# The last up unit of a routed block as three products of rounded high and low parts

## The chip, the cores and the metric

The kernel runs on one core of a Trainium2 chip. The metric is the device time of one execution, in microseconds; lower is better. A core has TensorE (matmuls; PE in the profile, with its weight loads as PEld), VectorE (DVE), ScalarE (ACT), GpSimd (POOL) and SyncE (SP), which here only issues DMAs. Each engine runs its own instructions in order and waits for others by semaphores.

## The reference, cut to what matters

A cross attention and a self attention come first, and then a feed-forward layer with experts on 512 tokens of width 512. Two shared experts see every token; of eight routed experts each token sees two.

```python
def _gelu(x):
    return jax.nn.gelu(x, approximate=False)
sh = _gelu(jnp.einsum('td,sdh->sth', xf, sW1) + sb1[:, None, :])
...
gates = xf @ rW + rb
topk_vals, topk_idx = jax.lax.top_k(gates, TOP_K)
...
h = _gelu(jnp.einsum('td,edh->eth', xf, W1) + b1[:, None, :])
y = jnp.einsum('eth,ehd->etd', h, W2) + b2[:, None, :]
moe = jnp.einsum('te,etd->td', w, y)
```

All of it is in float32. The kernel computes `h` and `y` only for the chosen pairs of token and expert, gathered into blocks of 128 rows of one expert each.

## The kernel before, in words

**Numbers.** TensorE takes float32 operands in two ways here. A plain float32 matmul is issued as two instructions, each with its own load of the stationary 128x128 tile. The other way uses the rounded type float32r (`F32R`), whose matmul is one instruction. To keep the precision, an operand is then split into a high part, the value cast to float32r, and a low part, the value less its high part, and a product is made of three terms: high by high, high by low, low by high. In the trace both kinds are printed as f32. Which is which is seen from the line and the tiles: `wsh`/`wsl`, `hh`/`hl`, `xAh`/`xAl`, `xBh`/`xBl`, `blk`, `wkh`/`wkl` and `wvh`/`wvl` are parts in float32r.

**Stages.** Attention fills the span up to about 770 us, then come the shared experts (lines 1146 and 1166, two passes over 256 tokens each), and from 971 us the routed blocks, one after the other, up to 1231 us. There can be up to `NBLK` = 15 blocks; `NE` = 8 are run always, the others behind a branch on the number of blocks, and this input runs 10.

**One routed block k.** Its 2 x 4 weight units of 1 MB each (128 partitions of 2048 floats) go through `ring`, eight buffers, of which unit n takes number n % 8. So up unit q of every block lies in buffer q, and down unit q in buffer 4 + q. SyncE loads them in the order up 0 to 3, down 0 to 3 (`load_block`, line 620), an up unit when PE has finished with that buffer's up unit of the block before (`ru_pe`), a down unit when DVE has split the one before (`wl_dve`).

- Up: for each unit q PE makes 4 output tiles of 4 matmuls (line 1285), stationary 128x128 pieces of the unit as they came in, moving the 128 gathered tokens `xg` (part of `xT`). ACT applies the GELU with the bias (line 1507), DVE splits the result into `hTh` and `hTl` (lines 2020, 2022). The up phase uses banks 0 and 1 in turn.
- Between: PE transposes the gathered rows of the next block (`turn_fetched`, line 1206), DVE copies them out of the bank into `xg` (`fetched`, line 1921).
- Down: for each unit q, 4 x 3 matmuls with 512 moving columns (line 1302), from `wsh`/`wsl`, the parts of the down unit: high by ACT (`weights_hi`, line 1378), low by DVE (`weights_split`, line 1721). ACT then scales the result (line 1518) into `yr`, or from block 7 on into `yh`.
- GpSimd only issues the indirect DMAs: it stores the rows of block k (`store`, line 843) and fetches the rows of block k + 3 (`fetch`, line 829). From block 8 on PE adds the block before into the result by a selection matmul (line 1263), behind up unit 0.

After block 6's rows are stored, SyncE reads all stored rows back, and only then loads the units of block 8.

Of the kernel before, what the change touches and what calls it, by code (L numbers as in the profile page):

```python
# [5 lines left out]
F32 = mybir.dt.float32  # L6
# [175 lines left out]
def build(nc, x, ctx, tails, wq, bq, wk, bk, wv, bv, wo, bo, ak, av, aq, ap_, abp, rw, rb,  # L182
          w1, b1, w2, b2, out):
    st = ExitStack()
    with st:
        def sb(name, shape, dt=F32):
            return st.enter_context(nc.sbuf_tensor(name, shape, dt))
# [111 lines left out]
        with ExitStack() as over:  # L299
# [28 lines left out]
        wsh2, wsl2 = sb("wsh2", [P, 2048], F32R), sb("wsl2", [P, 2048], F32R)  # L328
        ring1 = sb("ring1", [P, 2048])
        xBl = sb("xBl", [P, 4, 256], F32R)  # L330
        ring3 = sb("ring3", [P, 2048])
        xr = sb("xr", [P, 2, D])
        ring0, ring5 = sb("ring0", [P, 2048]), sb("ring5", [P, 2048])
# [10 lines left out]
        hTl = hl[:, :, :].rearrange("p a (b k) -> p (a b) k", b=4)  # L344
        yh = xAh[:, 0:2, :].rearrange("p b k -> p (b k)")
        yl = xAl[:, 0:2, :].rearrange("p b k -> p (b k)")

        xg = xT[:, 2:4, :].rearrange("p a (t k) -> p a t k", t=4)
        iotaw = xT[:, 0, :].bitcast(I32)
# [16 lines left out]
            "eps_dve iota_dve ones_dve cs_dve un_dve wkl_dve wvl_dve tl_dve kt_dve bias_dve xr_dve f_dve "  # L366
            "cr_dve bn_dve xn_dve xa_dve xt_dve sm_dve oh_dve nrm_dve xl_dve rt_dve hd_dve "
            "zero_dve wide_dve wl_dve xg_dve gt_dve rh_dve yl_dve add_dve last_dve sum_dve "
            "const_pool mask_pool iota_pool unit_pool cl_pool da_pool k2_pool bp_pool wide_pool xa_pool nm_pool wol_pool xl_pool wql_pool wsum_pool wsl_pool"
        ).split()  # L370
        s = {n: st.enter_context(nc.semaphore(n)) for n in names}
        bank_read = [st.enter_context(nc.semaphore(f"bank{i}_read")) for i in (0, 1, 7)]
# [3 lines left out]
        wq_in = [st.enter_context(nc.semaphore(f"wq{c}_in")) for c in range(2)]  # L376
        x_in = [st.enter_context(nc.semaphore(f"x{h}_in")) for h in range(2)]
        ring_in = [st.enter_context(nc.semaphore(f"ring{i}_in")) for i in range(NR)]
        b1_in = [st.enter_context(nc.semaphore(f"b1_{k}_in")) for k in range(NBLK)]

        pj = [bank[0], bank[1], bank[7]]
        uses = projections()
# [39 lines left out]
        def slot(n):  # L422
            return n % NR
# [61 lines left out]
        def sync(e):  # L485
# [133 lines left out]

            def load_block(k):  # L620
                ex = e.value_load(kint[0:1, k:k + 1], min_val=0, max_val=7)
                e.dma_start(b1r[:, k, :], b1[ex]).then_inc(b1_in[k], 16)
                for kind in (0, 1):
                    for q in range(4):
                        n = unit_routed(k, q, kind)
                        wait_slot(n)
                        e.dma_start(ring[slot(n)][:], (w1, w2)[kind][ex, q]).then_inc(ring_in[slot(n)], 16)
# [20 lines left out]
        def pool(e):  # L648
# [172 lines left out]
            def fetch(k):  # L821

                if k == 0:
                    e.wait_ge(s["rt_dve"], RT_TAB)
                    e.wait_ge(s["rows_in"], 64)
                    e.wait_ge(s["pr_pe"], 4)
                elif k >= 2:
                    e.wait_ge(s["tg_pe"], k - 1)
                e.indirect_dma_start(xr[:, k % 2, :], None, xrows,
                                     bass.IndirectOffsetOnAxis(ap=tabi[:, 0, k:k + 1], axis=0)).then_inc(s[("even_in", "odd_in")[k % 2]], 16)  # L830

            def fetch_rest(k):
                if k < NBLK:
                    with e.If(blocks > k - 1):
                        fetch(k)
                        fetch_rest(k + 1)

            def store(k):

                e.wait_ge(s["yh_act"], k + 1)  # L840
                if k == 0:
                    e.wait_ge(s["yz_in"], 16)
                e.indirect_dma_start(yrows, bass.IndirectOffsetOnAxis(ap=tabi[:, 1, k:k + 1], axis=0), yr[:, k % 2, :],  # L843
                                     None).then_inc(s[("even_out", "odd_out")[k % 2]], 16)

            for k in range(3):
                fetch(k)
            for k in range(NDIR):
                store(k)
                if k + 3 <= NE:  # L850
                    fetch(k + 3)
            fetch_rest(NE + 1)

        def pe(e):
            def warm(n, dst):
# [341 lines left out]
            def turn_fetched(k):  # L1197
                e.wait_ge(s[("even_in", "odd_in")[k % 2]], 16 * (k // 2) + 16)
                if k == 0:
                    e.wait_ge(s["wT_act"], 1)  # L1200
                elif k == 1:
                    e.wait_ge(s["ge_act"], 2 * NSH)
                else:
                    e.wait_ge(s["xg_dve"], k)
                for c in range(4):
                    m = e.transpose(bank[3 if k else 1][:, P * c:P * c + P], xr[:, k % 2, P * c:P * c + P], ident[:])
                m.then_inc(s["tg_pe"], 1)
# [60 lines left out]
            def routed(k):  # L1268
                y = k % 2
                for q in range(4):  # L1270
                    un = unit_routed(k, q, 0)
                    if q == 1 and k > NDIR:
                        e.wait_ge(s["yl_dve"], k - NDIR)
                        e.wait_ge(s["gt_dve"], k - NDIR)
                        scattered("sc_pe")
                    if 4 * k + q >= 2:
                        e.wait_ge(s["rg_act"], 4 * k + q - 1)
                    else:
                        e.wait_ge(s["rt_dve"], RT_POS)
                    e.wait_ge(ring_in[slot(un)], ring_value(un))  # L1280
                    if q == 0:
                        e.wait_ge(s["xg_dve"], k + 1)
                    for jj in range(4):
                        for c in range(4):
                            m = e.matmul(bank[q % 2][:, P * jj:P * jj + P],  # L1285
                                         ring[slot(un)][:, 512 * c + P * jj:512 * c + P * jj + P], xg[:, y, c, :],
                                         start=(c == 0), stop=(c == 3))
                    m.then_inc(s["ru_pe"], 1)
                if k + 1 < NBLK:
                    turn_fetched(k + 1)  # L1290
                if k == 0:
                    e.wait_ge(s["ge_act"], 2 * NSH)
                elif k <= NDIR:
                    e.wait_ge(s["yh_act"], k)
                for q in range(4):
                    r_ = 32 + 4 * k + q
                    e.wait_ge(s["rh_dve"], 2 * (4 * k + q) + 2)
                    e.wait_ge(s["wl_dve"], r_ + 1)
                    for jj in range(4):
                        j = 4 * q + jj  # L1300
                        for x_, (h_, w_) in enumerate(((hTh, wsh), (hTh, wsl), (hTl, wsh))):
                            m = e.matmul(bank[2][:], h_[:, j, :], w_[r_ % 3][:, 512 * jj:512 * jj + 512],  # L1302
                                         start=(j == 0 and x_ == 0), stop=(j == 15 and x_ == 2))
                    m.then_inc(s["rd_pe"], 1)
# [13 lines left out]
        def act(e):  # L1318
# [172 lines left out]
            e.wait_ge(s["rt_dve"], RT_INT)  # L1491
            blocks = e.value_load(kint[0:1, 15:16], min_val=0, max_val=NBLK)

            def routed(k):
                y = k % 2
                for q in range(4):
                    if q < 3:
                        weights_hi(32 + 4 * k + q)
                    n = 4 * k + q
                    e.wait_ge(s["ru_pe"], n + 1)  # L1500
                    if n >= 2:
                        e.wait_ge(s["rh_dve"], 2 * (n - 2) + 2)
                    if q == 0:
                        e.wait_ge(b1_in[k], 16)
                    for jj in range(4):
                        j = 4 * q + jj
                        m = e.activation(hg[:, q % 2, P * jj:P * jj + P], bank[q % 2][:, P * jj:P * jj + P], ACT.Gelu,
                                         bias=b1r[:, k, j:j + 1])
                    m.then_inc(s["rg_act"], 1)
                weights_hi(32 + 4 * k + 3)  # L1510
                e.wait_ge(s["rd_pe"], 4 * k + 4)
                if k == 0:
                    e.wait_ge(s["tab_in"], 16)
                elif 2 <= k <= NDIR + 1:
                    e.wait_ge(s[("even_out", "odd_out")[k % 2]], 16 * (k // 2))
                if k > NDIR:
                    e.wait_ge(s["sc_pe"], k - NDIR)
                e.activation(yr[:, y, :] if k < NDIR else yh, bank[2][:], ACT.Identity, scale=tab[:, k, 1:2]).then_inc(s["yh_act"], 1)  # L1518

            def rest(k):  # L1520
                if k < NBLK:
                    with e.If(blocks > k):
                        routed(k)
                        rest(k + 1)

            for k in range(NE):
                routed(k)
            rest(NE)
# [11 lines left out]
        def vector(e):  # L1540
# [375 lines left out]
            def fetched(k):  # L1916
                y = k % 2
                e.wait_ge(s["tg_pe"], k + 1)
                if k >= 2:
                    e.wait_ge(s["ru_pe"], 4 * (k - 2) + 4)  # L1920
                e.tensor_copy(xg[:, y, :, :],
                              bank[3 if k else 1][:].rearrange("p (c k) -> p c k", c=4)).then_inc(s["xg_dve"], 1)

            for n in range(NSLOT):
                i, d = part_of(n) if n < NCH else (NPART, 0)
# [115 lines left out]
            def rest(k):  # L2041
                if k < NBLK:
                    with e.If(blocks > k):
                        routed(k)
                        rest(k + 1)
# [70 lines left out]
```

## Time and profile before

| | |
|---|---|
| time, median of 3 runs | 1240.17 us (1238.33 to 1241.58) |
| the profiled execution's own time | 1241.11 us |
| its span, first to last instruction | 1239.4 us |
| mean granted TensorE clock | 0.991 |
| PE busy | 1210.2 us, 98% of the span |
| DVE, ACT, POOL busy | 68%, 55%, 46% |
| DMA queues of weights and data | 172.42 MB, 38.0% of 16 engines over the span |

The shares are means over stages with different limits; POOL, for instance, is busy in the attention and nearly idle in the last quarter. The difference of 1.7 us between time and span lies outside the profiled instructions.

### The profile page before, as it was taken

The page shows a single profiled execution, that of the slowest core. Times are in us where ns is not written, and L with a number is a line of the kernel's source. Part 1 is how long each engine was busy: PE and PEld are TensorE (multiplying, and loading weights), DVE is VectorE, ACT ScalarE, POOL GpSimd, SP SyncE. Part 2 cuts the span into 40 slices and gives each one's busy share as a digit, 9 for nine tenths or more (in the row PEclk, how much of TensorE's full clock was granted, in tenths as well). Part 3 has the DMA queues.
Part 4 walks back from the last instruction along what each step waited for, and adds up shares of the span by engine and source line. Part 5 has one row for each costly group of instructions (what it writes and reads, how often), then busy time and mean ns, then how long its engine had stood idle before and what let it go on. Part 6 is the DMA issues. An engine that isn't in the chain of part 4 may idle for free.

```text
span 1239.4 us, 33792 instructions
## 1 busy us (share of the span) xinstructions
PE 1210.2 (98%) x14478; PEld 1133.6 (91%) x14478; DVE 839.8 (68%) x1265; ACT 687.0 (55%) x1236; POOL 571.7 (46%) x357
## 2 busy tenths in 40 slices
PE   8999999999999999999999998999999999999998
PEld 7899999989999989999989997898889999999997
DVE  7666786776777686786785875766676455555655
ACT  4366656745755655756656557555644445544443
POOL 5656767776758776867766764000041001000000
PEclk9999999999999999999999998899999999999999
DMA  7331111121121212012112123745455599999991
GB/s 268 121 105 40 41 40 37 44 73 67 41 82 39 76 70 70 23 67 74 41 70 74 36 107 146 306 172 179 170 191 208 192 362 345 346 338 354 355 384 36
DMA packets 34794, 179.40 MB, mean 145 GB/s; under 512 B 6264, under 2 KB 9496, under 8 KB 15568
## 3 DMA queue, kind: packets, MB, share of 16 engines
q1 hardware_dynamic: 32896, 172.42, 38.0%
q0 software_dynamic: 1744, 4.76, 1.2%
q8 instruction: 117, 1.92, 0.6%
q14 instruction: 37, 0.30, 0.1%
HBM read 168.97 MB, written 8.19 MB: 143 GB/s over the span
## 4 chain that ended last, share of the span: by engine, by line
PE 91%; DVE 4%; issue 2%; POOL 1%; ACT 1%; DMA 0%; DVEq 0%; SPq 0%; POOLq 0%
PE bank L928 18%; PE bank L931 18%; PE bank L1285 12%; PE sc L1302 9%; PE sc L951 7%; PE sc L1146 7%; PE bank L970 4%; PE sc L1166 4%; PE bank L1166 4%; PE bank L909 1%; PE bank L1037 1%; DVE tt L1623 1%; POOL xn L731 1%; PE bank L1091 1%; PE bank L996 1%
## 5 line engine op out<-in xcount | busy, mean ns | idle before, releaser
L731 POOL TENSOR_TENSOR xn<-xn,tt 128x1024 f32<-128x1024 f32 x96 | 231.9, 2416 | 165.1 <-DVE tt L1623 163.3
L931 PE MATMUL bank<-wvh,blk 128*128 128x256 f32 x1344 | 248.8, 287 | 5.3 <-DVE va L1594 5.3
L928 PE MATMUL bank<-blk,wkh 128*128 128x256 f32 x1344 | 246.0, 285 | 0.0
L1721 DVE TENSOR_TENSOR wsl<-ring,wsh 128x2048 fp32r<-128x2048 f32 x72 | 165.2, 2294 | 112.6 <-ACT wsh L1378 109.8
L1442 ACT ACTIVATE tt<-sc 128x512 f32<-128x512 f32 (+1 forms) x208 | 107.8, 603 | 217.1 <-PE sc L951 209.3
L931 PEld LDWEIGHTS bank<-wvh,blk 128*128 128x128 f32 x1344 | 209.9, 192 | 8.8 <-DVE va L1594 6.1
L928 PEld LDWEIGHTS bank<-blk,wkh 128*128 128x128 f32 x1344 | 209.2, 192 | 4.2 <-issue 1.6
L931 PE MATMUL bank<-wvl,blk 128*128 128x256 f32 x672 | 190.6, 284 | 0.0
L928 PE MATMUL bank<-blk,wkl 128*128 128x256 f32 x672 | 190.0, 283 | 0.0
L1378 ACT CAST wsh<-ring 128x2048 fp32r<-128x2048 f32 x72 | 137.4, 1909 | 45.8 <-PE sc L1302 21.2
L1285 PEld LDWEIGHTS bank<-xT,ring 128*128 128x128 f32 x1280 | 144.8, 192 | 1.0
L1285 PE MATMUL bank<-xT,ring 128*128 128x128 f32 x1280 | 144.8, 275 | 0.0
L1623 DVE SCALAR_TENSOR_TENSOR tt<-sc,tt 128x512 f32<-128x512 f32 (+1 forms) x208 | 132.9, 680 | 0.8 <-ACT tt L1455 0.8
L931 PEld LDWEIGHTS bank<-wvl,blk 128*128 128x128 f32 x672 | 129.4, 193 | 0.0
L928 PEld LDWEIGHTS bank<-blk,wkl 128*128 128x128 f32 x672 | 128.8, 192 | 0.0
L685 POOL TENSOR_TENSOR blk<-bsum,blk 128x512 fp32r<-128x512 f32 x96 | 124.1, 1321 | 6.1 <-DVE bsum L1572 4.8
L1451 ACT ACTIVATE tt<-tt 128x512 f32<-128x512 f32 (+1 forms) x208 | 121.2, 644 | 0.0
L1455 ACT ACTIVATE tt<-tt 128x512 f32<-128x512 f32 (+1 forms) x208 | 120.9, 643 | 0.0
L951 PEld LDWEIGHTS sc<-qc,kk 32*128 32x128 f32 x3072 | 91.7, 189 | 11.9 <-DVE tt L1623 4.3
L951 PE MATMUL sc<-qc,kk 32*128 32x64 f32 x3072 | 98.3, 276 | 4.1 <-DVE tt L1623 4.1
L685 POOL TENSOR_TENSOR blk<-stg,blk 128x512 fp32r<-128x512 f32 x72 | 97.1, 1362 | 1.8 <-ACT blk L1330 1.8
L843 POOL DMA_INDIRECT yrows<-xT,tabi x7 | 6.9, 988 | 193.2 <-ACT xT L1518 193.2
(327 smaller groups left out, 2204.9 us busy)
## 6 DMA issues: line engine op xcount, KB each, us to landing
ring<-in_w SPq DMA_DIRECT2D x112, 1024.0 KB, 6.1
stg<-in_ctx SPq DMA_DIRECT2D x24, 1024.0 KB, 5.0
wqt<-in_wo SPq DMA_DIRECT2D x4, 1024.0 KB, 5.0
wqt<-in_aq SPq DMA_DIRECT2D x4, 1024.0 KB, 5.0
wqt<-in_ap_ SPq DMA_DIRECT2D x4, 1024.0 KB, 4.9
yrows<-K SPq DMA_DIRECT2D x1, 2048.0 KB, 12.4
bsum<-in_tails SPq DMA_DIRECT2D x2, 520.0 KB, 6.6
ktail<-bsum SPq DMA_DIRECT2D x1, 1040.0 KB, 4.1
```

The source lines that it names most:

```text
L685: e.tensor_tensor(block_lo(i, j), block_raw(i, j), block_hi(i, j).bitcast(F32), ALU.subtract).then_inc(s["cl_pool"], 1)
L731: e.tensor_tensor(dacc[0:kn, y, :], dacc[0:kn, y, :], tt[0:kn, w, :], ALU.add).then_inc(s["da_pool"], 1)
L928: m = e.matmul(dst[:, 256 * a:256 * a + 256], w[:, WPOS[j], c, r], x[:, c, :], start=(k_ == 0), stop=(k_ == 5))
L931: m = e.matmul(dst[:, 256 * a:256 * a + 256], x[:, c, r], w[:, WPOS[j], c, :], start=(k_ == 0), stop=(k_ == 5))
L951: m = e.matmul(sc[0:kn, h, c0 + 64 * g:c0 + 64 * g + 64], key, qc[r, g, 64 * b:64 * b + 64], start=True, stop=True)
L1285: m = e.matmul(bank[q % 2][:, P * jj:P * jj + P], ring[slot(un)][:, 512 * c + P * jj:512 * c + P * jj + P], xg[:, y, c, :], start=(c == 0) ...
L1302: m = e.matmul(bank[2][:], h_[:, j, :], w_[r_ % 3][:, 512 * jj:512 * jj + 512], start=(j == 0 and x_ == 0), stop=(j == 15 and x_ == 2))
L1378: e.copy(wsh[m % 3][:], ring[slot(un)][:]).then_inc(s["wh_act"], 1)
L1451: e.activation(tt[0:kn, w, r], tt[0:kn, w, r], ACT.Ln, bias=1.0).then_inc(s["ln_act"], 1)
L1455: e.activation(tt[0:kn, w, r], tt[0:kn, w, r], ACT.Exp, scale=-1.0).then_inc(s["ex_act"], 1)
L1623: e.scalar_tensor_tensor(t_, score_read(n, kn, hb), 0.0, t_, ALU.max, ALU.add).then_inc(s["f_dve"], 1)
L1721: e.tensor_tensor(wsl[m % 3][:], ring[slot(unit_split(m))][:], wsh[m % 3][:].bitcast(F32), ALU.subtract).then_inc(s["wl_dve"], 1)
```

## The change

In every routed block the last up unit (q = 3) is multiplied in three terms of float32r parts, where it was one plain float32 product. Three things are made for that.

- The high part of the unit, `uph`, by ACT: two casts of 128x1024 into `xBh` and `xBl`, the buffers of the shared experts' second pass (`up_hi`). For blocks below 8 it is made one block ahead, behind the cast of down unit 3; for block 0 at the start of the stage; for blocks 8 and later at the start of the block itself.
- The low part, `upl`, by GpSimd: two subtractions of 128x1024, written over ring buffer 3 itself, in which the raw unit lies (`up_lo`). GpSimd does it for block k + 1 ahead of the store of block k.
- The parts of the 128 gathered tokens, `xgh` and `xgl`, by DVE from the bank, behind the copy into `xg`, which the units 0 to 2 still use.

The bias loads of the blocks take two semaphores, by the block's parity, in place of fifteen.

```diff
+            upl = over.enter_context(nc.sbuf_tensor("upl", [P, 2048], F32R))
         ring3 = sb("ring3", [P, 2048])
...
+        xgh, xgl = (w[:, 2:4, :].rearrange("p a (t k) -> p (a t) k", t=2) for w in (xAh, xAl))
+        uph = [w[:, :, :].rearrange("p c k -> p (c k)") for w in (xBh, xBl)]
...
-                e.dma_start(b1r[:, k, :], b1[ex]).then_inc(b1_in[k], 16)
+                e.dma_start(b1r[:, k, :], b1[ex]).then_inc(b1_in[k % 2], 16)
...
+            def up_lo(k):
+
+                e.wait_ge(s["uph_act"], k + 1)
+                for h in range(2):
+                    c = slice(1024 * h, 1024 * h + 1024)
+                    m = e.tensor_tensor(upl[:, c], ring[slot(unit_routed(k, 3, 0))][:, c], uph[h].bitcast(F32), ALU.subtract)
+                m.then_inc(s["upl_pool"], 1)
...
+            up_lo(0)
+            for k in range(NE):
+                if k + 1 < NE:
+                    up_lo(k + 1)
+                if k < NDIR:
+                    store(k)
                 if k + 3 <= NE:
                     fetch(k + 3)
...
                     if q == 0:
-                        e.wait_ge(s["xg_dve"], k + 1)
+                        e.wait_ge(s["xg_dve"], 3 * k + 1)
+                    elif q == 3:
+                        e.wait_ge(s["xg_dve"], 3 * k + 3)
+                        e.wait_ge(s["upl_pool"], k + 1)
                     for jj in range(4):
+                        dst = bank[q % 2][:, P * jj:P * jj + P]
                         for c in range(4):
...
+                            if q < 3:
+                                m = e.matmul(dst, ring[slot(un)][:, col], xg[:, y, c, :], start=(c == 0), stop=(c == 3))
+                                continue
+                            hi = uph[c // 2][:, 512 * (c % 2) + P * jj:512 * (c % 2) + P * jj + P]
+                            for x_, (w_, x__) in enumerate(((hi, xgh), (hi, xgl), (upl[:, col], xgh))):
+                                m = e.matmul(dst, w_, x__[:, c, :], start=(c == 0 and x_ == 0), stop=(c == 3 and x_ == 2))
...
+            def up_hi(k):
+
+                un = unit_routed(k, 3, 0)
+                e.wait_ge(ring_in[slot(un)], ring_value(un))
+                for h in range(2):
+                    m = e.copy(uph[h], ring[slot(un)][:, 1024 * h:1024 * h + 1024])
+                m.then_inc(s["uph_act"], 1)
...
                 weights_hi(32 + 4 * k + 3)
+                if k + 1 < NE:
+                    up_hi(k + 1)
                 e.wait_ge(s["rd_pe"], 4 * k + 4)
...
+                e.tensor_copy(xg[:, y, :, :], src).then_inc(s["xg_dve"], 1)
+                e.tensor_copy(xgh, src).then_inc(s["xg_dve"], 1)
+                e.wait_ge(s["xg_dve"], 3 * k + 2)
+                e.tensor_tensor(xgl, src, xgh.bitcast(F32), ALU.subtract).then_inc(s["xg_dve"], 1)
```

On TensorE, at the up phase of block 1, the order before is (each row is a line, an operation, the tile written and the tiles read, the moving shape and a count):

```order
L1302 MATMUL sc<-wsh,hl 128x512
L1285 MATMUL bank<-xT,ring 128x128 x64
L1206 MATMUL sc<-ident,xr 128x128 x4
L1302 MATMUL sc<-wsh,hh 128x512
L1302 MATMUL sc<-wsl,hh 128x512
```

And of the change, at the same place (its lines 1309, 1313, 1224 and 1328 are the plain up matmuls, the new ones, the transposes and the down matmuls):

```order
L1328 MATMUL sc<-wsh,hl 128x512
L1309 MATMUL bank<-xT,ring 128x128 x48
L1313 MATMUL bank<-xAh,xBh 128x128
L1313 MATMUL bank<-xAl,xBh 128x128
L1313 MATMUL bank<-xAh,upl 128x128
...
L1224 MATMUL sc<-ident,xr 128x128 x4
L1328 MATMUL sc<-wsh,hh 128x512
```

The three new rows stand 16 times in all (with `xBl` in the place of `xBh` for half of them): the last 16 of the 64 plain matmuls are gone, and 48 of float32r stand in their place, still 128 moving columns wide.

On ScalarE, in block 0, from the cast of down unit 3 into block 1, before:

```order
L1507 ACTIVATE hr<-bank,K 128x128 x8
L1378 CAST wsh<-ring 128x2048
L1518 ACTIVATE xT<-sc,tab 128x512
L1378 CAST wsh<-ring 128x2048
L1507 ACTIVATE hr<-bank,K 128x128 x4
```

And of the change:

```order
L1543 ACTIVATE hr<-bank,K 128x128 x8
L1404 CAST wsh<-ring 128x2048
L1525 CAST xBh<-ring 128x1024
L1525 CAST xBl<-ring 128x1024
L1556 ACTIVATE xT<-sc,tab 128x512
L1404 CAST wsh<-ring 128x2048
```

The two casts of `up_hi` for block 1 have come in ahead of the scaling of block 0's result.

On GpSimd, behind the three fetches that open the stage, before:

```order
L829 DMA xr<-xrows,tabi 128x512 x3
L843 DMA yrows<-xT,tabi 2944x512
L829 DMA xr<-xrows,tabi 128x512
L843 DMA yrows<-xT,tabi 2944x512
L829 DMA xr<-xrows,tabi 128x512
```

And of the change:

```order
L833 DMA xr<-xrows,tabi 128x512 x3
L857 TENSOR_TENSOR upl<-ring,xBh 128x1024
L857 TENSOR_TENSOR upl<-ring,xBl 128x1024
L857 TENSOR_TENSOR upl<-ring,xBh 128x1024
L857 TENSOR_TENSOR upl<-ring,xBl 128x1024
L849 DMA yrows<-xT,tabi 2944x512
L833 DMA xr<-xrows,tabi 128x512
```

The subtractions for blocks 0 and 1 now stand ahead of the store of block 0, and so on by one pair for each block.

## Rows read from the trace of the kernel before

**Rows 1.** The page: busy us of each engine, and the chain that ended last by line.
```profile
PE 1210.2 (98%) x14478; PEld 1133.6 (91%) x14478; DVE 839.8 (68%) x1265; ACT 687.0 (55%) x1236; POOL 571.7 (46%) x357
PE bank L928 18%; PE bank L931 18%; PE bank L1285 12%; PE sc L1302 9%; PE sc L951 7%; PE sc L1146 7%; PE bank L970 4%; PE sc L1166 4%; PE bank L1166 4%; PE bank L909 1%; PE bank L1037 1%; DVE tt L1623 1%; POOL xn L731 1%; PE bank L1091 1%; PE bank L996 1%
```

**Rows 2.** The chain in order of time, blocks 1 and 8: start us, length us, count.
```profile
996.87 14.29 PE bank L1285 x128
1011.16 0.44 PE sc L1206 x4
1011.60 10.93 PE sc L1302 x48
...
1176.49 3.57 PE bank L1285 x32
1181.93 10.72 PE bank L1285 x96
```

**Rows 3.** Busy time in block 1: length, engines, granted clock, DMA share.
```profile
core 0: us, PE busy (x) PEld busy (x) DVE busy (x) ACT busy (x) POOL busy (x), PEclk, DMA share, GB/s
996.87:1022.53 25.66, 25.66 (x183) 23.74 (x182) 14.01 (x13) 12.52 (x21) 1.96 (x2) 1.00 0.92 349
```

**Rows 4.** Groups by line and shape, the up matmuls: busy us, mean ns.
```profile
L1285 PE MATMUL bank<-xT,ring 128*128 128x128 f32 x1280 | 144.8, 275 | 0.0
```

**Rows 5.** Chain: float32r matmuls 256 columns wide in the shared experts.
```profile
925.96 2.75 PE bank L1166 x12
928.71 2.87 PE sc L1146 x24
```

**Rows 6.** Timeline of weight loads: start, us, out<-in, stationary shape, count.
```profile
374.11 0.98 PEld L1014 LDWEIGHTS bank<-rwt,xaT 128*128 128x128 f32 x8
375.01 0.30 PEld L928 LDWEIGHTS bank<-blk,wkh 128*128 128x128 f32 x2
...
884.42 0.17 PEld L1181 LDWEIGHTS bank<-sel,ones 128*128 128x128 bf16 x4
...
6.93 0.66 PEld L857 LDWEIGHTS bank<-ones 128*128 128x128 bf16 x11
...
1011.33 0.19 PEld L1302 LDWEIGHTS sc<-wsh,hh 128*128 128x128 f32 x1
1011.44 0.19 PEld L1302 LDWEIGHTS sc<-wsl,hh 128*128 128x128 f32 x1
```

**Rows 7.** The weight loads of line 1181: ns min/median/max.
```profile
L1181 PEld LDWEIGHTS bank<-sel,ones x4: 95/96/96, 884.4 to 884.5; 128*128 128x128 bf16 x4
```

**Rows 8.** Timeline of ACT and DVE, block 1, between up and down.
```profile
1013.45 0.68 DVE L1921 COPY xT<-sc 128x512 f32<-128x512 f32 x1
1014.46 1.91 ACT L1378 CAST wsh<-ring 128x2048 fp32r<-128x2048 f32 x1 [2.12 <-PE sc L1302]
1016.40 2.29 DVE L1721 TENSOR_TENSOR wsl<-ring,wsh 128x2048 fp32r<-128x2048 f32 x1 [2.28 <-ACT wsh L1378]
1022.57 0.69 ACT L1518 ACTIVATE xT<-sc,tab 128x512 f32<-128x512 f32 x1 [6.20 <-PE sc L1302]
```

**Rows 9.** Prices from other stages: an ACT cast, DVE and POOL operations.
```profile
L1413 ACT CAST woh<-wqt 128x1024 fp32r<-128x1024 f32 x2 | 2.0, 1038 | 0.0
L1639 DVE TENSOR_TENSOR xTl<-sc,xTh 128x512 fp32r<-128x512 f32 x4 | 2.6, 681 | 0.2 <-ACT xTh L1346 0.2
L731 POOL TENSOR_TENSOR xn<-xn,tt x96: 2347/2405/4258, 78.2 to 771.9; 128x1024 f32<-128x1024 f32 x88, 65x1024 f32<-65x1024 f32 x8
```

**Rows 10.** Ring loads, issue to landing: 990 to 1050, then 1150 to 1185 us.
```profile
DMA to landing us min/median/max: 4.8/6.4/8.1
...
DMA to landing us min/median/max: 6.6/11.0/14.1
```

**Rows 11.** Timeline of POOL in block 2, and of ACT in block 8.
```profile
1023.53 0.99 POOL L843 DMA_INDIRECT yrows<-xT,tabi  x1 [23.40 <-ACT xT L1518]
...
1179.81 1.91 ACT L1378 CAST wsh<-ring 128x2048 fp32r<-128x2048 f32 x1 [2.60 <-DMA ring<-in_w]
```

More of the change, by code:

```diff
@@ L330, in build @@
         xBl = sb("xBl", [P, 4, 256], F32R)
+        with ExitStack() as over:
+            upl = over.enter_context(nc.sbuf_tensor("upl", [P, 2048], F32R))
         ring3 = sb("ring3", [P, 2048])
@@ L368, in build @@
             "zero_dve wide_dve wl_dve xg_dve gt_dve rh_dve yl_dve add_dve last_dve sum_dve "
-            "const_pool mask_pool iota_pool unit_pool cl_pool da_pool k2_pool bp_pool wide_pool xa_pool nm_pool wol_pool xl_pool wql_pool wsum_pool wsl_pool"
+            "const_pool mask_pool iota_pool unit_pool cl_pool da_pool k2_pool bp_pool wide_pool xa_pool nm_pool wol_pool xl_pool wql_pool uph_act upl_pool wsum_pool wsl_pool"
         ).split()
@@ L378, in build @@
         ring_in = [st.enter_context(nc.semaphore(f"ring{i}_in")) for i in range(NR)]
-        b1_in = [st.enter_context(nc.semaphore(f"b1_{k}_in")) for k in range(NBLK)]
+        b1_in = [st.enter_context(nc.semaphore(f"b1_{k}_in")) for k in range(2)]
         pj = [bank[0], bank[1], bank[7]]
@@ L830, in fetch, with rest @@
                                      bass.IndirectOffsetOnAxis(ap=tabi[:, 0, k:k + 1], axis=0)).then_inc(s[("even_in", "odd_in")[k % 2]], 16)
-            def fetch_rest(k):
+            def rest(k):
                 if k < NBLK:
-                    with e.If(blocks > k - 1):
-                        fetch(k)
-                        fetch_rest(k + 1)
+                    with e.If(blocks > k):
+                        if k + 1 < NBLK:
+                            fetch(k + 1)
+                        up_lo(k)
+                        rest(k + 1)
             def store(k):
@@ L844, in store @@
                                      None).then_inc(s[("even_out", "odd_out")[k % 2]], 16)
+            def up_lo(k):
[4 more added lines that the diff above has]
+                m.then_inc(s["upl_pool"], 1)
             for k in range(3):
                 fetch(k)
-            for k in range(NDIR):
-                store(k)
+            up_lo(0)
[4 more added lines that the diff above has]
+                    store(k)
                 if k + 3 <= NE:
                     fetch(k + 3)
-            fetch_rest(NE + 1)
+            rest(NE)
         def pe(e):
@@ L1203, in turn_fetched @@
                 else:
-                    e.wait_ge(s["xg_dve"], k)
+                    e.wait_ge(s["xg_dve"], 3 * k)
                 for c in range(4):
@@ L1281, in routed @@
                     if q == 0:
-                        e.wait_ge(s["xg_dve"], k + 1)
+                        e.wait_ge(s["xg_dve"], 3 * k + 1)
+                    elif q == 3:
+                        e.wait_ge(s["xg_dve"], 3 * k + 3)
+                        e.wait_ge(s["upl_pool"], k + 1)
                     for jj in range(4):
+                        dst = bank[q % 2][:, P * jj:P * jj + P]
                         for c in range(4):
-                            m = e.matmul(bank[q % 2][:, P * jj:P * jj + P],
-                                         ring[slot(un)][:, 512 * c + P * jj:512 * c + P * jj + P], xg[:, y, c, :],
-                                         start=(c == 0), stop=(c == 3))
+                            col = slice(512 * c + P * jj, 512 * c + P * jj + P)
+                            if q < 3:
[4 more added lines that the diff above has]
+                                m = e.matmul(dst, w_, x__[:, c, :], start=(c == 0 and x_ == 0), stop=(c == 3 and x_ == 2))
                     m.then_inc(s["ru_pe"], 1)
@@ L1492, in act @@
             blocks = e.value_load(kint[0:1, 15:16], min_val=0, max_val=NBLK)
+            def up_hi(k):
[4 more added lines that the diff above has]
+                m.then_inc(s["uph_act"], 1)
             def routed(k):
                 y = k % 2
+                if k >= NE:
+                    up_hi(k)
                 for q in range(4):
@@ L1503, in routed @@
                     if q == 0:
-                        e.wait_ge(b1_in[k], 16)
+                        e.wait_ge(b1_in[k % 2], 16 * (k // 2 + 1))
                     for jj in range(4):
@@ L1524, in rest @@
                         rest(k + 1)
+            up_hi(0)
             for k in range(NE):
@@ L1920, in fetched @@
                     e.wait_ge(s["ru_pe"], 4 * (k - 2) + 4)
-                e.tensor_copy(xg[:, y, :, :],
-                              bank[3 if k else 1][:].rearrange("p (c k) -> p c k", c=4)).then_inc(s["xg_dve"], 1)
+                src = bank[3 if k else 1][:].rearrange("p (c k) -> p c k", c=4)
+                e.tensor_copy(xg[:, y, :, :], src).then_inc(s["xg_dve"], 1)
+                e.tensor_copy(xgh, src).then_inc(s["xg_dve"], 1)
+                e.wait_ge(s["xg_dve"], 3 * k + 2)
+                e.tensor_tensor(xgl, src, xgh.bitcast(F32), ALU.subtract).then_inc(s["xg_dve"], 1)
             for n in range(NSLOT):
```

## The prediction

> **What bounds the kernel now.** I read the page first. TensorE is busy 98% of the span, and the chain that ended last lies on it almost throughout; lines 1285 and 1302, the up and down matmuls of the routed blocks, hold 12% and 9% [rows 1]. The chain in order of time then shows how a block is made up: 14.29 us of up matmuls, 0.44 us of transposes, 10.93 us of down matmuls, one behind the other without a gap, 25.66 us in all [rows 2]. The busy times of block 1 say the same from the other side: PE 25.66 of 25.66 us at a granted clock of 1.00, which is 2.4 GHz, while DVE works 14.01, ACT 12.52 and POOL 1.96 us [rows 3]. So a microsecond more or less on TensorE counts once for every block, and work on the other engines counts only if it makes TensorE wait. 1280 up instructions [rows 4] at 128 to a block [rows 2] are 10 blocks. One thing stands near: the DMA engines are busy 0.92 of a block, moving 349 GB/s [rows 3]. A much shorter block would meet that; a longer one loosens it.
>
> **What TensorE loses and gains.** An up phase has 128 instructions in 14.29 us, 111.6 ns each, so unit 3, a quarter of them (16 matmuls of two instructions), takes 3.57 us. In its place come 48 float32r matmuls, 128 columns wide, each with its own load of a 128x128 stationary tile. No such matmul is in the trace: its float32r matmuls are 256 wide or wider. Their rates are the nearest rows. 24 matmuls 256 wide take 2.87 us, 119.6 ns each; 12 that are 512 wide take 2.75 us, 229 ns each [rows 5]; 48 in a down phase take 10.93 us, 228 ns [rows 2]. The step from 256 to 512 columns costs 108 ns, that is 2.4 columns a ns, and about 12 ns are left over for each matmul. By that line alone 128 columns would take 53 + 12 = 65 ns. The 48 would take 3.1 us, and a block would win 0.45 us.
>
> [...] The gate's matmuls on line 1014 have only 8 moving columns, next to nothing to stream. Still their eight loads go from 374.11 to the next line's start at 375.01, 0.90 us, or 112 ns for each [rows 6]. So for a plain float32 tile the load is the bound, at 112 ns, which is also the 111.6 ns of the up phase. Is it the same for float32r? The first two loads of a down phase, float32r tiles with nothing in front of them, start 110 ns apart, at 1011.33 and 1011.44, while the later ones follow the matmuls' 228 ns [rows 6]. So a float32r tile, four bytes an element too, loads at 110 ns, and the loads, not the 53 ns of streaming, should set the pace of the new unit. bf16 tiles show how else it could be: four loads of a 128x128 bf16 tile end 0.17 us after the first began [rows 6] and last 0.095 us each [rows 7], so they start 25 ns apart; the eleven of line 857, for matmuls 128 wide, take 0.66 us, (0.66 - 0.10) / 10 = 56 ns apart [rows 6].
>
> Bounds for one new matmul with a load as the bound: 110 ns from the two loads, below; 119.6 ns above, the 256-wide float32r rate, since half the columns can't take longer. I take 112 ns, the pace of a chain that is seen to be bound by loads. It is nearest in what sets it; the 119.6 ns contain 107 ns of streaming, which the new unit has not. Then the unit takes 48 x 0.112 = 5.38 us, 1.80 us more than 3.57, and 10 blocks take **18.0 us** more. With 110 ns it is 48 x 0.110 - 3.57 = 1.71, 17.1 us; with 119.6 ns 5.74 - 3.57 = 2.17, 21.7 us.
>
> The Trainium skill, in TensorE: Matmul & The Clock Gate, section Back-to-back issue gap, states about 81 ns for each pair of a load and a matmul with 128 columns in a stream. By it the unit would take 3.89 us and the change cost 3.2 us. The trace has 112 ns where a four-byte tile is loaded, and I go by that.
>
> **ACT.** A cast of 128x1024 takes 1.04 us [rows 9], so `up_hi` adds 2.1 us to 12.52 of a block. In block 1 the cast of down unit 3 ends at 1016.37, and ACT idles 6.20 us before it scales the result at 1022.57 [rows 8]. There it waits for the next block's unit 3. SyncE can issue that load when the up phase ends, at 1011.16, and loads land 4.8 to 8.1 us after issue [rows 10]: at 1019.3 at the latest. The two casts end by 1021.4, before 1022.57. Cost nothing. If the load came more than 1.2 us later than that, the scaling, the next block's first cast and its first GELU would slip; but that GELU is needed only when the third up unit wants its bank, 7.1 us into the block.
>
> **GpSimd.** A subtraction of 128x1024 takes 2.4 us [rows 9], two 4.8. From 1021.4 they end by 1026.2; unit 3 of the next block is due at 1022.53 + 10.7 = 1033.2 by the old times. 7 us of cover. Behind them on GpSimd stand the store of the block's rows, issued at 1023.53 now [rows 11], up to 2.7 us later then, and the fetch for two blocks on. The store's reader is the reuse of `yr` two blocks later. The last one matters more: SyncE reads all rows back after store 6 and has the loads of block 8 behind that. There ACT waits 2.60 us for the ring, and casts the first down unit only at 1179.81 [rows 11], 3.3 us into block 8; the landings take up to 14.1 us [rows 10]. In blocks 8 and 9 `up_hi` comes ahead of that cast. If its unit landed only with the down unit, ACT would be done with it at 1181.9 and GpSimd at 1186.7; unit 3 is due at 1181.93 + 7.15 = 1189.1. The down unit's cast would end at 1183.8, and the first GELU, 1.14 us, at 1184.9, where the third up unit needs its bank at 1181.93 + 3.57 = 1185.5. It just fits, and each earlier block being longer gives loads more time. I put 0 here, with 1 us at most.
>
> **DVE.** Two operations follow the copy at 1013.45, a cast and a subtraction from a bank of 0.68 us each [rows 8, 9]. They end near 1015.5; the split of down unit 3 starts at 1016.40, held by ACT's cast [rows 8]. Nothing, with 0.9 us of cover; beyond it down unit 3, which comes at 1011.60 + 8.2 = 1019.8, has 1.1 us more behind the split's end at 1018.7. Block 0's operations fall in the shared experts, where TensorE is the bound too.
>
> **Semaphores and SyncE.** SyncE's order of loads is the same, and the parity wait asks for a load that was issued a block earlier. Nothing.
>
> Sum: 1241.11 + 18.0 = 1259.1 us against the profiled execution; that lies 0.9 above the median of the runs, so the median becomes **1258 us**.
>
> **Rivals.**
>
> *The load is hidden, and the change is faster.* If float32r tiles load faster in a row than the one pair shows, the unit goes by its streaming: 65 ns by the line above, 0.45 us won a block, 1235.7 us; with the 56 ns of the bf16 chain 2.69 us, 0.88 won, 1231.4 us. It decides below 74 ns a matmul, where 48 equal 3.57 us. For it: 12 + 53 fits every wider matmul. Against: the 110 ns pair, the 112 ns of line 1014. Chance 0.07. With the page's 81 ns it would be 1243.4 us, inside what a measurement can tell from no change; 0.03.
>
> *A narrow float32r matmul has a price that the wide ones don't show.* If it took as long as the two instructions of a plain float32 product, 223 ns, the unit would take 10.7 us, 7.1 more a block, 1312 us. Nothing in the trace speaks for it, and nothing is narrow enough to exclude it. 0.05.
>
> *The parts come late.* TensorE at its first new matmul waits for GpSimd. It costs what the chain ring, ACT, GpSimd exceeds 7 us of cover by, or 2.4 us in block 8. If GpSimd were three times as slow beside DVE (a single 4.26 us in [rows 9] is the slowest of 96), 2 x 7.2 = 14.4 us are 2.6 us over, 10 blocks 26 us, 1284 us. 0.03.
>
> **How the numbers follow.** The load-bound case has 0.82 and its own range from 1257 (110 ns) to 1263 us (119.6 ns, with the 1 us of block 8). About 0.3%, 3.7 us, is what a measurement tells from no change. Faster is the hidden load, 0.06 of its 0.07, since at 65 ns the gain is near that bound; the same 0.04; slower 0.90. The range: 1253 to 1266 us, which takes the load-bound case with 3 us to spare on either side for unpriced seams, and leaves out the others, 0.18.
>
> **What would show each step.** The new matmuls' group: 48 in 5.4 us, starting 112 ns apart; transposes and down phase unchanged at 0.44 and 10.93 us; a block of 27.5 us instead of 25.66; before unit 3 no wait for POOL or DVE; POOL about 5 us busier a block; DMA share below 0.92. Starts 60 to 70 ns apart, or a wait of TensorE for `upl`, would make the prediction wrong.

## The result, and the profile after

The change takes 1258.62 us, the median of 4 runs (1257.23 to 1259.45), against 1240.33 us for the kernel before in the same comparison. The ratio is 1.0146 with a 95% interval of 1.0131 to 1.0161: 18 us slower. The profiled execution took 1258.62 us, with a span of 1256.7.

The chain in order of time, block 1 and block 8 of the changed kernel (start us, length us, what; lines 1309, 1313, 1224 and 1328 are the plain up matmuls, the new ones, the transposes and the down matmuls), to be held against [rows 2]:

```profile
998.68 10.72 PE bank L1309 x96
1009.40 5.31 PE bank L1313 x48
1014.71 0.46 PE sc L1224 x4
1015.17 10.92 PE sc L1328 x48
1026.10 10.72 PE bank L1309 x96
1036.81 5.31 PE bank L1313 x48
...
1190.58 3.57 PE bank L1309 x32
1196.02 7.14 PE bank L1309 x64
1203.16 5.31 PE bank L1313 x48
```

The pieces still follow each other without a gap (in block 8 the selection matmuls of line 1281 fill the 1.87 us between 1194.15 and 1196.02). The three plain units keep 10.72 us, the 48 new matmuls take 5.31 us, 110.6 ns each, where the plain unit took 3.57. The blocks start 27.42 us apart, where they were 25.66 apart, so a block is 1.76 us longer; ten blocks make 17.6 us, and the span grew by 17.3. The busy times of block 1, against [rows 3]:

```profile
core 0: us, PE busy (x) PEld busy (x) DVE busy (x) ACT busy (x) POOL busy (x), PEclk, DMA share, GB/s
998.68:1026.10 27.42, 27.42 (x199) 25.50 (x198) 15.30 (x15) 14.43 (x23) 6.92 (x5) 1.00 0.86 326
```

TensorE is busy all the time at full clock. ACT has 1.9 us more, GpSimd 5.0, DVE 1.3, and the DMA share has fallen from 0.92 to 0.86, because the same megabytes go over a longer block.

The weight loads of the new matmuls, and one of the matmuls, from the timeline in block 1 (start us, length us):

```profile
1009.13 0.19 PEld L1313 LDWEIGHTS bank<-xAh,xBh 128*128 128x128 f32 x1
1009.24 0.19 PEld L1313 LDWEIGHTS bank<-xAl,xBh 128*128 128x128 f32 x1
1009.30 0.28 PE L1313 MATMUL bank<-xAl,xBh 128*128 128x128 f32 x1
1009.35 0.19 PEld L1313 LDWEIGHTS bank<-xAh,upl 128*128 128x128 f32 x1
1009.46 0.19 PEld L1313 LDWEIGHTS bank<-xAh,xBh 128*128 128x128 f32 x1
```

One load starts every 0.11 us. Each is recorded with 0.19 us, and its matmul's record starts before the load's ends (1009.30 against 1009.43), so loads overlap each other and their matmuls. What this document calls the cost or the pace of a load is the spacing of their starts, not the length of one. Even where the stationary tile stays the same (`xBh` under `xAh` and then under `xAl`) it is loaded anew.

ACT, DVE and GpSimd around the same place, against [rows 8, 11]:

```profile
1018.03 1.92 ACT L1404 CAST wsh<-ring 128x2048 fp32r<-128x2048 f32 x1 [2.13 <-PE sc L1328]
1019.84 1.05 ACT L1525 CAST xBh<-ring 128x1024 fp32r<-128x1024 f32 x1
1020.78 1.05 ACT L1525 CAST xBl<-ring 128x1024 fp32r<-128x1024 f32 x1
1026.13 0.69 ACT L1556 ACTIVATE xT<-sc,tab 128x512 f32<-128x512 f32 x1 [4.30 <-PE sc L1328]
...
1018.31 0.69 DVE L1964 TENSOR_TENSOR xAl<-sc,xAh 128x512 fp32r<-128x512 f32 x1
1019.98 2.29 DVE L1760 TENSOR_TENSOR wsl<-ring,wsh 128x2048 fp32r<-128x2048 f32 x1 [0.97 <-ACT wsh L1404]
...
1021.92 2.60 POOL L857 TENSOR_TENSOR upl<-ring,xBh 128x1024 fp32r<-128x1024 f32 x1 [19.96 <-ACT xBl L1525]
1024.49 2.38 POOL L857 TENSOR_TENSOR upl<-ring,xBl 128x1024 fp32r<-128x1024 f32 x1
1027.10 1.00 POOL L849 DMA_INDIRECT yrows<-xT,tabi  x1 [0.23 <-ACT xT L1556]
```

ACT still idles 4.30 us before it scales the result, DVE 0.97 us before the split of down unit 3, GpSimd has the low part ready at 1026.87, and TensorE comes to the next block's unit 3 only at 1036.81. The store goes out behind the scaling at 1027.10, not held by the subtractions. In block 8 the raw unit had landed when ACT came to it:

```profile
1191.20 1.03 ACT L1525 CAST xBh<-ring 128x1024 fp32r<-128x1024 f32 x1
1192.14 1.04 ACT L1525 CAST xBl<-ring 128x1024 fp32r<-128x1024 f32 x1
1193.08 1.91 ACT L1404 CAST wsh<-ring 128x2048 fp32r<-128x2048 f32 x1
1194.89 1.13 ACT L1543 ACTIVATE hr<-bank,K 128x128 f32<-128x128 f32 x4
...
1195.62 4.40 POOL L857 TENSOR_TENSOR upl<-ring,xBl 128x1024 fp32r<-128x1024 f32 x1
```

The slow second subtraction ends at 1200.02, 3.1 us before TensorE wants it at 1203.16.

### The profile page after: what moved, and what is told of

It reads as the page before. It is cut to its first block, busy times and chain, and to the rows that moved or that the text cites. A ratio compares the mean times of both kernels' runs of the same rounds, so it can differ in the third digit from the quotient of the medians.

```text
span 1256.7 us, 34184 instructions
## 1 busy us (share of the span) xinstructions
PE 1227.3 (98%) x14638; PEld 1151.3 (92%) x14638; DVE 859.8 (68%) x1287; ACT 705.9 (56%) x1256; POOL 627.1 (50%) x377
## 4 chain that ended last, share of the span: by engine, by line
PE 92%; DVE 4%; issue 2%; POOL 1%; ACT 1%; DMA 0%; DVEq 0%; SPq 0%; POOLq 0%
PE bank L946 18%; PE bank L949 18%; PE sc L1328 9%; PE bank L1309 9%; PE sc L969 7%; PE sc L1164 7%; PE bank L1313 4%; PE bank L988 4%; PE sc L1184 4%; PE bank L1184 4%; PE bank L927 1%; PE bank L1055 1%; DVE tt L1662 1%; POOL xn L735 1%; PE bank L1109 1%
## 5 line engine op out<-in xcount | busy, mean ns | idle before, releaser
L857 POOL TENSOR_TENSOR upl<-ring,xBh 128x1024 fp32r<-128x1024 f32 x10 | 25.3, 2535 | 210.6 <-ACT xBl L1525 210.6
L1309 PEld LDWEIGHTS bank<-xT,ring 128*128 128x128 f32 x960 | 109.0, 192 | 1.0
L1309 PE MATMUL bank<-xT,ring 128*128 128x128 f32 x960 | 109.1, 275 | 0.0
```

The lines of the kernel that those rows point to most:

```text
L1309: m = e.matmul(dst, ring[slot(un)][:, col], xg[:, y, c, :], start=(c == 0), stop=(c == 3))
```

## The experiments

The theory: loads of 128x128 stationary tiles of four-byte elements start no closer than about 111 ns apart at the full clock; the new unit has 48 such loads where the plain one has 32, and that is the whole of the 18 us. The rivals: narrow float32r matmuls stream slowly; part of the loss is preparation and waits; the number of matmuls counts whatever the format.

**Fewer columns: 64, then 96.**

```diff
-                                m = e.matmul(dst, w_, x__[:, c, :], start=(c == 0 and x_ == 0), stop=(c == 3 and x_ == 2))
+                                m = e.matmul(dst[:, 0:64], w_, x__[:, c, 0:64], start=(c == 0 and x_ == 0), stop=(c == 3 and x_ == 2))
```

> The new matmuls of the change move 64 columns in place of 128; half of the last up unit's products are left out, all else is the change. Theory (each load of a 128x128 four-byte tile sets the pace, about 111 ns): the 48 matmuls still take 5.3 us and the time stays at 1258.6 us. Rival (a float32r matmul with few columns streams at half rate, 1.16 columns a ns, so that the 110.6 ns are streaming): the 48 take about 2.7 to 3.4 us and the time falls by about 20 to 26 us.

Measured: 1287.09 us, ratio 1.0381 (1.0363 to 1.0399). Neither expectation fits: half the columns made the kernel 28 us slower than the change. The timeline of weight loads in block 0 and the busy times of its plain up units, its new unit and its down phase (PE, clock, DMA share, GB/s) show what happened:

```profile
985.80 0.19 PEld L1313 LDWEIGHTS bank<-xAh,upl 128*128 128x128 f32 x1
985.91 0.27 PEld L1313 LDWEIGHTS bank<-xAh,xBh 128*128 128x128 f32 x1
986.06 0.34 PEld L1313 LDWEIGHTS bank<-xAl,xBh 128*128 128x128 f32 x1
986.28 0.33 PEld L1313 LDWEIGHTS bank<-xAh,upl 128*128 128x128 f32 x1
986.49 0.33 PEld L1313 LDWEIGHTS bank<-xAh,xBl 128*128 128x128 f32 x1
```

```profile
971.11:981.83 10.72, 10.72 (x99) 1.00 0.49 172
981.83:988.02 6.19, 6.19 (x49) 0.83 0.62 216
988.95:1001.74 12.79, 12.79 (x51) 0.85 0.97 379
```

Up to 985.8 the loads start 0.11 us apart, exactly as with 128 columns, so the columns do not set the pace; the half-rate rival is out. Then the granted clock falls to its lower level, 1.2 GHz, within the new unit, and the loads start 0.21 us apart: from 986.28 to the last one at 987.56 they are 0.213 us apart in the mean. So a load takes about twice as long at half the clock. The down phase starts at the low clock and takes 12.79 us in place of 10.93. This came back in every block: the ten new units took 5.64 to 7.23 us. The clock stood in neither expectation; to have the load alone, the same edit was run with 96 columns.

> As the run with 64 columns, but the new matmuls move 96 of their 128; a quarter of the last up unit's products are left out. Asks whether the 28 us that the run with 64 columns lost come from the granted clock, which fell there, or from the load. Theory (load sets the pace at the full clock; the clock falls only where TensorE's columns get too few): at 96 columns the clock stays at 1.00 in the blocks, the 48 take 5.3 us, 1258.6 us. Rival (narrow float32r matmuls lower the clock as such): the clock falls below 0.9 here too, and the time rises above 1265 us.

Measured: 1270.82 us, ratio 1.0271 (1.0207 to 1.0334), the four runs at 1260.82, 1263.74, 1277.89 and 1279.16. In the profiled one, 1260.82 us, nine blocks kept the clock at 1.00 and one did not. Its chain, in block 4 and in block 8:

```profile
1079.72 10.72 PE bank L1309 x96
1090.44 5.30 PE bank L1313 x48
...
1201.96 6.53 PE bank L1313 x48
1208.48 0.90 PE sc L1224 x4
1209.38 12.48 PE sc L1328 x48
```

5.30 us with 96 columns, 5.31 with 128: the load is the bound. Of the clock neither expectation was right as a whole: it stayed at 1.00 in nine blocks, but fell in one, and the median lies above the 1265 us of the rival. The one fall cost 1.23 + 0.43 + 1.55 = 3.2 us. The mean granted clocks of the four runs, in the order of their times, are 0.990, 0.988, 0.975 and 0.974, which fits more such falls in the slower two; where these lay is not known, since only one run was profiled.

**More columns: 256.**

```diff
-                                m = e.matmul(dst, w_, x__[:, c, :], start=(c == 0 and x_ == 0), stop=(c == 3 and x_ == 2))
+                                m = e.matmul(bank[q % 2][:, P * min(jj, 2):P * min(jj, 2) + 256], w_, (xAh, xAl)[x_ == 1][:, 2 + c // 2, :], start=(c == 0 and x_ == 0), stop=(c == 3 and x_ == 2))
```

> The new matmuls move 256 columns in place of 128, over neighbouring output tiles, so the last up unit's values are not those of the reference. Theory (the larger of a 111 ns load and streaming plus 12 ns): 48 x 119.6 ns = 5.74 us, 0.43 more a block, 1262.9 us. Rival (half rate at few columns alone): the same 5.74 us, since 256 columns are seen to take 119.6 ns elsewhere; rival (load and streaming add up): 48 x (111 + 53) = 7.9 us, 1284 us.

Measured: 1260.67 us, ratio 1.0157 (1.014 to 1.0174). From the chain in order of time:

```profile
1008.84 5.70 PE bank L1313 x48
1014.54 0.44 PE sc L1224 x4
```

48 matmuls take 5.70 us, 118.8 ns each. Twice the columns cost 0.39 us in a unit; the sum of load and streaming, 7.9 us, is out. This agrees with the larger of the two setting the pace. (The half-rate rival names the same 5.74 us here; it is the 64 and 96 columns that rule it out.)

**Two terms in place of three.**

```diff
-                            for x_, (w_, x__) in enumerate(((hi, xgh), (hi, xgl), (upl[:, col], xgh))):
...
+                            for x_, (w_, x__) in enumerate(((hi, xgh), (upl[:, col], xgh))):
```

> The term high by low is left out of the last up unit: 32 matmuls in place of 48, all preparation as in the change. Theory (the cost is the number of loads): 32 x 110.6 ns = 3.54 us, as long as the plain unit of before: 1240.6 us, no measurable difference to before. Rival (part of the 18 us comes from the new preparation or its waits): above 1243 us.

Measured: 1240.4 us over 10 runs, ratio 1.0 (0.9991 to 1.001). With as many loads as the plain unit, 32, the unit takes as long (chain in order of time):

```profile
1007.94 3.52 PE bank L1313 x32
```

All 18 us are gone with 16 of the 48 matmuls.

**The plain matmuls with 64 columns,** in the kernel before.

```diff
-                            m = e.matmul(bank[q % 2][:, P * jj:P * jj + P],
-                                         ring[slot(un)][:, 512 * c + P * jj:512 * c + P * jj + P], xg[:, y, c, :],
+                            m = e.matmul(bank[q % 2][:, P * jj:P * jj + 64],
+                                         ring[slot(un)][:, 512 * c + P * jj:512 * c + P * jj + P], xg[:, y, c, 0:64],
```

> The kernel before, with 64 moving columns in all of its plain float32 up matmuls; half of the up products are left out. Theory (the load is the bound of the plain matmuls too): the up phase stays at 14.3 us and the time at 1240.3 us. Rival (the plain matmul is bound by streaming its 128 columns twice): the up phase falls towards 8 us, and the time by 30 us or more, until GELU, splits or DMA hold it.

Measured: 1240.71 us over 10 runs, ratio 1.0003 (0.9993 to 1.0012). The up phase, from the chain:

```profile
997.46 14.24 PE bank L1285 x128
```

14.24 us against 14.29 in [rows 2]: the plain matmuls are bound by their loads too. So an instruction of either kind costs a load, and the exchange was 48 loads for 32. The clock did not fall here, with 64 columns in all four units: it was 1.00 from 971 to 1231 us.

**The preparation alone.**

```diff
-                    m = e.tensor_tensor(upl[:, c], ring[slot(unit_routed(k, 3, 0))][:, c], uph[h].bitcast(F32), ALU.subtract)
+                    m = e.tensor_tensor(uph[h], ring[slot(unit_routed(k, 3, 0))][:, c], uph[h].bitcast(F32), ALU.subtract)
...
-                            if q < 3:
+                            if q < 4:
```

> All preparation of the change is made (high part by ACT, low part by GpSimd, the tokens' parts by DVE, and TensorE's waits for them), but the last up unit is multiplied plain, as before; the low part is written over the high part and used by nothing. Theory (the preparation is hidden): 1240.3 us, within 1 us of before. Rival (part of the cost is preparation, ring release or DMA timing): the part of the 18 us that it makes, above 1242 us.

Measured: 1240.14 us over 10 runs, ratio 1.0003 (0.9991 to 1.0016), the up phase as before (from the chain):

```profile
997.25 14.29 PE bank L1309 x128
```

Casts, subtractions, waits and semaphores cost nothing that can be measured in a block of this length.

**bf16 parts.** The same three terms with all four parts in bf16, the moving ones too. The low part lies in a buffer of its own and no longer over the ring.

```diff
+        with ExitStack() as over:
+            uphb = over.enter_context(nc.sbuf_tensor("uphb", [P, 2048], BF16))
         xBh = sb("xBh", [P, 4, 256], F32R)
...
+            upl = over.enter_context(nc.sbuf_tensor("upl", [P, 2048], BF16))
         xBl = sb("xBl", [P, 4, 256], F32R)
-        with ExitStack() as over:
-            upl = over.enter_context(nc.sbuf_tensor("upl", [P, 2048], F32R))
...
+        xgh, xgl = (xgb[:, 1024 + 512 * a:1536 + 512 * a].rearrange("p (c k) -> p c k", c=4) for a in range(2))
+        uph = [uphb[:, 1024 * a:1024 * a + 1024] for a in range(2)]
```

> The change with the four parts (uph, upl, xgh, xgl) in bf16 in place of float32r, 48 matmuls as in the change; the low part lies in a buffer of its own and no longer over the ring. The products of the last up unit are less precise than in float32r. Theory (the pace is the load of a four-byte tile; bf16 tiles load 25 ns apart): 48 x 56 ns = 2.7 us in place of 5.31, 26 us less than the change, 1232 us, and 0.9 us a block less than before. Rival (the number of matmuls or their order sets the pace, whatever the format): 5.3 us and 1258.6 us.

Measured: 1231.9 us, ratio 0.9931 (0.9907 to 0.9956): 27 us below the change and 8 below the kernel before. From its chain (line 1317 is the new unit there), and one group of its matmuls by line and shape (busy us, mean ns):

```profile
1006.73 2.68 PE bank L1317 x48
1009.41 0.45 PE sc L1228 x4
```

```profile
L1317 PE MATMUL bank<-xgb,upl 128*128 128x128 bf16 x160 | 27.3, 219 | 0.0
```

The same 48 matmuls over the same 128 columns, 56 ns each. The number of matmuls is not the cost; the format is. This run changes the format of the stationary and of the moving tiles together. That it is the stationary ones that count follows from the runs with 64 and 96 columns, where fewer moving columns left the 0.11 us as they were.

**The operands swapped.** The tokens' tile stands still, 512 columns of the unit move. The result is not turned back.

```diff
+                    if q == 3:
+                        for c in range(4):
+                            hi, lo = uph[c // 2][:, 512 * (c % 2):512 * (c % 2) + 512], upl[:, 512 * c:512 * c + 512]
+                            for x_, (x__, w_) in enumerate(((xgh, hi), (xgl, hi), (xgh, lo))):
+                                m = e.matmul(bank[q % 2][:], x__[:, c, :], w_, start=(c == 0 and x_ == 0), stop=(c == 3 and x_ == 2))
+                    for jj in range(4 if q < 3 else 0):
```

> The same three float32r terms of the last up unit with the operands' roles swapped: the tokens' 128x128 tile is stationary and 512 columns of the unit move, 12 loads and 12 matmuls in place of 48. The result lands turned, tokens by hidden units, and is not turned back, so the values that GELU sees are not those of the reference, and four transposes and a copy that a full version needs are left out. Theory (cost is the load unless streaming is longer): 12 x 228 ns = 2.74 us in place of 5.31, 25.7 us less than the change, 1232.9 us. Rival (the three terms themselves cost, whatever carries the columns): 1258.6 us.

Measured: 1234.07 us, ratio 0.9957 (0.994 to 0.9974). From the chain:

```profile
1005.26 2.80 PE bank L1308 x12
1008.06 0.44 PE sc L1224 x4
```

2.80 us for 12 matmuls, 233 ns each, 5 more than assumed. So float32r can win on this unit if each load carries 512 columns. A full version would add at least four transposes, 0.44 us like the row below, and a copy out of a bank, to turn the result; by this estimate 2.80 + 0.44 = 3.24 us is still below 3.57, by 3 us over ten blocks, if the copy is hidden. It was not built.

In this shorter block something else shows: TensorE waited once, 1.0 us in block 7, for DVE's split of the last down unit. The chain leads from there back to a ring load issued behind the read-back of the stored rows, to the store of block 6, and to GpSimd's subtractions ahead of that store:

```profile
1141.86 2.73 POOL upl L857 x2
...
1146.74 4.61 DMA yrows<-xT,tabi
...
1158.20 15.65 DMA ring<-in_w
```

ACT had scaled the result at 1144.51, but the subtractions ran to 1146.58 and the store was issued at 1146.74: about 2 us of the delay are GpSimd's. The prediction had looked at this path and put it at nothing for the longer block of the change; in this shorter one the preparation stands in the chain. No run shows whether the 1.0 us would be gone without it.

**bf16 in the down phase too,** on top of the bf16 version.

```diff
-                        for x_, (h_, w_) in enumerate(((hTh, wsh), (hTh, wsl), (hTl, wsh))):
+                        for x_, (h_, w_) in enumerate(((hTh, wshb), (hTh, wslb), (hTl, wshb))):
...
-                e.copy(wsh[m % 3][:], ring[slot(un)][:]).then_inc(s["wh_act"], 1)
+                e.copy((wsh if m < 32 else wshb)[m % 3][:], ring[slot(un)][:]).then_inc(s["wh_act"], 1)
```

> On top of the version with bf16 parts for the last up unit, the down phase of the routed blocks takes bf16 parts too (wsh, wsl, hTh, hTl; 512 moving columns, 48 matmuls). Less precise than float32r. Theory (the 12 to 14 ns that every float32r matmul takes beyond its columns belong to the four-byte format): 48 x 216 ns = 10.4 us in place of 10.92, 0.55 a block, 1226.4 us. Rival (they belong to every change of the stationary tile): 228 ns a matmul still and 1231.9 us. Rival (another engine or DMA holds the shorter block of about 24.2 us): TensorE waits for the ring or DVE, 1228 us or more.

Measured: 1227.62 us, ratio 0.99 (0.9884 to 0.9917), the fastest version. The down phase of block 2 and a ring load of block 7 in the chain, the busy times of the down phase of block 1 (DMA share and GB/s last), and the one group that waited:

```profile
1032.58 10.36 PE sc L1352 x48
...
1153.74 15.58 DMA ring<-in_w
```

```profile
1008.38:1018.74 10.36, 10.36 (x51) 4.85 (x49) 5.30 (x6) 4.63 (x6) 1.99 (x1) 1.00 1.00 404
```

```profile
L1352 PE MATMUL sc<-wshb,hhb 128*128 128x512 bf16 x160 | 60.6, 379 | 1.2 <-DVE wslb L1784 1.2
```

216 ns a matmul against 228: 12 ns of each float32r matmul belong to the four-byte format; whether to the stationary or the moving tile this run can't tell. The time is 1.2 us above the expected one, and 1.2 us is what TensorE waited for DVE's split once, in block 7. The chain puts that down to a ring load issued behind the read-back, which took 15.58 us to land. The DMA engines are busy 1.00 of a down phase at 404 GB/s, where the kernel before has 0.96 at 384. A still shorter block would probably meet them first; no run shows that, and outside block 7 TensorE does not wait for them yet.

## Why the prediction was right

1258.62 us were measured, 1258 forecast, and by the steps that were given. That the two agree within 1 us is partly luck: the runs of the change spread over 2.2 us, and the main term was 0.6 us too large. The mechanism and its size are what was right. (The range's lower end, 1253, lies 4 us below the 1257 of the load-bound case, not 3; nothing hangs on it.)

- **The bound.** TensorE without a gap, before and after; 1.76 us a block times ten is the difference.
- **The new unit: 48 x 112 ns = 5.38 us.** It was 5.31, 110.6 ns. The estimate of 18.0 us for ten blocks stands against 17.4 from this term; the low bound, 110 ns from two neighbouring loads, was the nearer row. The transposes took 0.46 in place of 0.44 us, 0.2 us in all, which was not foreseen; why stays open.
- **Load, not streaming.** Shown: 64 columns at the full clock, 96 and 128 take the same; 256 take 118.8 ns; two terms cost as much as the plain unit; with bf16 tiles the same matmuls go at 56 ns. The rival of the hidden load was wrong for float32r: the unit took neither 3.1 us (65 ns) nor 2.69 (56 ns). Its second number came from bf16 tiles, and it is what the bf16 parts took, 2.68 us.
- **81 ns a pair.** The Trainium skill's figure for a load and a matmul with 128 columns, in TensorE: Matmul & The Clock Gate, section Back-to-back issue gap, met neither format here: 110.6 ns with float32r tiles, 56 ns with bf16 ones.
- **A price of narrowness.** None at 128 columns. At 64 and 96 there is one, but it is the granted clock that falls, and that was no rival in the prediction. It also bounds a step of the prediction: that half the columns can't take longer held from 256 to 128 (118.8 to 110.6 ns), but not from 128 to 64, where the unit grew from 5.31 to 5.64 us and more.
- **ACT, GpSimd, DVE at nothing.** Shown by the preparation alone, 1.0003. ACT's two casts and DVE's 0.97 us of idle time before the split came as worked out. That GpSimd would delay the store by up to 2.7 us was too careful: the block was 1.76 us longer, and the ring's unit landed earlier than its latest time, for the casts began at 1019.84, 5.1 us after the up phase. Block 8, where 0 to 1 us was allowed, cost nothing, though one subtraction took 4.40 us in place of 2.4; 3.1 us of cover were left.
- **DMA.** The share fell below 0.92, to 0.86, as said. In the fastest version it is 0.94 to 0.98 in each of blocks 1 to 4, the row that the prediction said a much shorter block would meet.

## What to carry to other kernels

Count the stationary tiles, not the columns: with 128 moving columns a plain float32 product has two loads and three float32r terms have three, so the unit took half as long again (5.31 against 3.57 us), whatever its streaming would save. In this kernel three terms were shorter than the plain unit where each load carried 512 columns (2.80 us, without turning the result back) or where the parts were bf16 (2.68 us), if the precision allows it. A row with few moving columns (here eight) shows the price of a load by itself; look for one before an exchange of formats.

## What the runs showed of the hardware

Fewer columns for the same loads can cost time: with 64 float32r columns the granted clock fell in every block, and the kernel went from 1258.6 to 1287.1 us; with 96 it fell in one block of the profiled execution. The spacing of loads of four-byte tiles goes with the clock: 111 ns at 2.4 GHz and about 213 ns at 1.2. With plain float32 matmuls of 64 columns, their instructions as far apart (14.24 us for 128, 111 ns each), the clock did not fall at all; what tells the two apart for the clock stays open.
